# Four of 32 product chunks move a row or two later in a batched graph kernel

## The reference

```python
Ws = 0.5 * (W + jnp.swapaxes(W, -1, -2))
A = jax.nn.sigmoid(U @ U.T)
K = Ws * A[None, :, :]
deg = jnp.maximum(K.sum(axis=-1), EPS)
d = jax.lax.rsqrt(deg)
K = K * d[:, :, None] * d[:, None, :]
return w_scale * jnp.einsum('bnm,bmc->bnc', K, x)
# and around it
x = _layernorm(x + _L0_gnn_ref(x, adj, L0_gnn_U, L0_gnn_w_scale), axis=-1)
```

## Time and profile before

| | us |
|---|---|
| median of 3 runs | 486.6 |
| lowest and highest run | 481.2, 488.73 |
| the profiled execution, its own time | 489.78 |
| its span in the profile | 487.9 |

### The profile page before, as it was taken

How to read it: one execution, slowest core, us unless ns; L and a number is a source line. 1 busy time by engine, 2 the same in 40 slices (tenths; PEclk the granted TensorE clock), 3 DMA queues, 4 the chain that set the end, 5 groups by cost and what they waited for, 6 DMA issues and landing times.

```text
span 487.9 us, 14490 instructions
## 1 busy us (share of the span) xinstructions
PE 447.6 (92%) x5318; PEld 236.5 (48%) x5318; DVE 417.0 (85%) x1154; ACT 209.9 (43%) x655; POOL 113.4 (23%) x133
## 2 busy tenths in 40 slices
PE   7888899999989999999999999799998999899893
PEld 6556344555435553565354554454445544455352
DVE  6897467899699988999899998799889998799745
ACT  3886232554335442554335532454434542444420
POOL 0000011003330225103330234103330225103452
PEclk9996699999999999999999999999999999989998
DMA  8999299986999799996999699976999689984012
GB/s 290 387 330 350 81 362 368 359 301 221 358 343 324 259 321 362 375 326 236 362 380 358 212 380 364 351 241 244 387 345 343 261 322 361 356 253 170 2 41 47
DMA packets 101387, 143.11 MB, mean 293 GB/s; under 512 B 35824, under 2 KB 35824, under 8 KB 101360
## 3 DMA queue, kind: packets, MB, share of 16 engines
q1 hardware_dynamic: 86496, 139.01, 80.7%
q10 hardware_dynamic: 14864, 3.74, 3.6%
HBM read 138.54 MB, written 4.19 MB: 293 GB/s over the span
## 4 chain that ended last, share of the span: by engine, by line
PE 61%; DMA 14%; DVE 12%; issue 8%; ACT 2%; SPq 1%; POOL 0%; DVEq 0%; POOLq 0%
PE yp L437 35%; DMA k<-in_adj_dram 14%; PE tw L395 10%; PE kt L395 9%; DVE k L666 6%; DVE k L677 3%; PE yp L535 3%; PE yp L470 2%; ACT k L559 1%; ACT gate L546 1%; SPq L251 1%; DVE deg_parts L677 1%; DMA h<-in_L_gnn_U_dram 1%; PE kt L481 1%; PE kt L535 0%
## 5 line engine op out<-in xcount | busy, mean ns | idle before, releaser
L559 ACT ACTIVATE k<-kt 128x512 f32<-128x512 f32 (+3 forms) x288 | 149.5, 524 | 234.1 <-PE kt L395 233.8
L437 PE MATMUL yp<-k,z 128*64 128x512 f32 x944 | 239.6, 615 | 4.9 <-DVE z L697 2.6
L666 DVE TENSOR_TENSOR k<-tw,k 128x512 f32<-128x512 f32 (+2 forms) x320 | 193.4, 604 | 41.9 <-PE tw L395 28.5
L677 DVE CUSTOM_DVE_ANT_0 k<-k,gate 128x512 f32<-128x512 f32 (+2 forms) x320 | 198.5, 620 | 0.0
L395 PEld LDWEIGHTS kt<-ident,k 64*128 64x128 f32 x1920 | 75.4, 142 | 86.3 <-issue 86.1
L395 PEld LDWEIGHTS tw<-ident,k 64*128 64x128 f32 x2176 | 83.5, 141 | 67.0 <-issue 65.7
L395 PE MATMUL kt<-ident,k 64*128 64x64 f32 x1920 | 94.2, 232 | 19.5 <-DVE deg_parts L677 13.5
L395 PE MATMUL tw<-ident,k 64*128 64x64 f32 x2176 | 101.7, 230 | 4.5 <-DMA k<-in_adj_dram 1.7
L437 PEld LDWEIGHTS yp<-k,z 128*64 128x64 f32 x944 | 56.4, 137 | 73.1 <-issue 60.0
L327 POOL TENSOR_TENSOR d<-deg,minus_half 128x4 f32<-128x4 f32 x32 | 32.5, 1015 | 222.1 <-DVE deg L687 221.4
L559 ACT ACTIVATION_READ_ACCUMULATOR k<-kt 128x1 f32 x288 | 57.2, 198 | 0.0
(11 more groups left out here) (53 smaller groups left out, 138.7 us busy)
## 6 DMA issues: line engine op xcount, KB each, us to landing
k<-in_adj_dram SPq DMA_DIRECT2D x128, 1024.0 KB, 7.4
xt<-in_x_dram ACTq DMA_DIRECT2D x7, 512.0 KB, 7.6
out_dram<-h SPq DMA_DIRECT2D x7, 512.0 KB, 7.0
xt<-in_x_dram SPq DMA_DIRECT2D x1, 512.0 KB, 14.5
out_dram<-k SPq DMA_DIRECT2D x2, 128.0 KB, 2.1
out_dram<-k SPq DMA_DIRECT2D x3, 64.0 KB, 1.7
h<-in_L_gnn_U_dram SPq DMA_DIRECT2D x1, 128.0 KB, 3.2
out_dram<-k ACTq DMA_DIRECT2D x1, 64.0 KB, 1.9
```

What stands on the lines that cost most here:

```text
L437: t = pe.matmul(yp[at:at + C, m // 2, :], z[:, n * G + c, :], K[(n, m)][:, c, :], start=(q == first_unit[m] and c == 0), stop=(q == last_u ...
L559: nc.scalar.activation(K[(j, i)][:, r, c0:UW].rearrange("p (c h e) -> p c h e", h=2, e=H), whole_rows(kt[:, 0:2, :], r % 2, (UW - c0) // P ...
L666: nc.vector.tensor_tensor(row, whole_rows(tw[:, tw_bank[g] // 2 * 2:tw_bank[g] // 2 * 2 + 2, :], g % 2, w // P), row, ALU.add).then_inc(su ...
L677: nc.vector.tensor_tensor_reduce(row, row, A[:, A_AT[g]:A_AT[g] + w], 1.0, 0.0, ALU.mult, ALU.add, deg_parts[:, i * G + r, j:j + 1]).then_ ...
```

## The change

Four numbers of the table change, one or two rows each: chunk 27 goes from row 56 to 58, chunk 28 from 59 to 60, chunk 29 from 61 to 62, and chunk 31, the last one, from 65 to 66. Chunk 30 stays in row 64.

```diff
-PRODUCT_ROWS = [29, 29, 32, 32, 33, 33, 35, 35, 38, 38, 39, 39, 42, 44, 44, 45, 45, 45, 46, 46, 46, 47, 50, 52, 54, 56, 56, 56, 59, 61, 64, 65]
+PRODUCT_ROWS = [29, 29, 32, 32, 33, 33, 35, 35, 38, 38, 39, 39, 42, 44, 44, 45, 45, 45, 46, 46, 46, 47, 50, 52, 54, 56, 56, 58, 60, 62, 64, 66]
```

## The result

| | before | changed |
|---|---|---|
| median, us | 485.64 (4 runs) | 500.0 (4 runs) |
| lowest and highest, us | 481.2, 488.73 | 497.02, 502.63 |
| profiled execution, its own time, us | 489.78 | 497.02 |
| its span, us | 487.9 | 495.2 |
| its mean granted clock | 0.971 | 0.982 |

The ratio is 1.0285, with a 95% interval of 1.023 to 1.034. The forecast was 494.7 us, 1.7% slower, with a range up to 499: the sign was right, the time lies outside. The two profiled executions lie only 7.2 us apart, because that of before, taken apart from its four runs, was slower than each of them, and that of the changed kernel was the fastest of its four. So the profiles show where time goes, and the runs how much it is.

What follows compares the result with a forecast made beforehand. VectorE and TensorE bound the kernel in turn, with row 68's unit load just in time. Late loads of +8.9 us less 0.8 gave +8.1 us on a median of 486.6: 494.7 us, 1.7% slower, range 486 to 499.

Steps and rivals of the forecast that it cites:

- What bounds the kernel: VectorE limits one stretch of each element, TensorE the next; unit (3,2)'s load for row 68 lands just as needed.
- the ring of TensorE, load, VectorE: TensorE's products lead to a load, then VectorE, then TensorE; a late load is passed on one for one.
- Chunk 31's shift of 1.30 us: Row 66's tw and y transposes delay chunk 31 and group 7's load issue by 1.30 us, bounds 1.2 to 1.5.
- The wait at row 68: VectorE's add of row 68 waits 1.0 to 1.5 us for its load in all seven elements.
- Chunk 27 and ScalarE at no cost: Group 6's later loads and ScalarE's later second y copy cost 0; uncovered, at most 6.3 and 0.7 us.
- The 0.8 us back from the transposes of row 60: VectorE gets these transposes a chunk earlier, saving waits of 0.48 and 0.32 us in two elements: -0.8 us.
- 7 x 1.3 - 0.2 = +8.9: Seven late loads for row 68, 1.3 us each, less 0.2 us spare: +8.9 us, bounds +8.2 to +10.3.
- the clock, which I costed at 0 behind row 70's wait: TensorE's new 1.3 us wait at row 70 was taken not to lower the clock: 0 us.
- much slower: Idle time at row 70 lowers the clock in each of 7 elements: 11.9 us more, 506.6 us; chance 0.06.
- faster: A shorter stretch without products before row 58's kt keeps the clock up; 482.4 us with the load hidden; chance 0.07.
- The hidden load: Row 68's load stays hidden, only the 0.8 us gain is left: 485.8 us, half hidden 490; chance 0.18.

Runs made afterwards that it cites:

- only31_prey: Only chunk 31 moved from row 65 to 66, ahead of the four y transposes, against the kernel before: ratio 1.0071.
- only31: Only chunk 31 moved from row 65 to 66, behind the y transposes, against the kernel before: ratio 1.0264.
- only27_29: Chunks 27, 28 and 29 moved as in the change, chunk 31 left in row 65, against the kernel before: ratio 1.0013.
- after_again: The changed kernel, unedited, timed and profiled a second time beside the kernel before: ratio 1.0261.

## Why the prediction was wrong, step by step

**What bounds the kernel**: right. The load of unit (3,2) was on the edge, and the ring of TensorE, load, VectorE passes a delay on one for one. In `only31_prey`, `only31` and the changed kernel row 70's `kt` waits as long as the add of row 68, within 0.04 us, in the six elements beside the second. From VectorE's add of row 40 to the same add an element later, the shortest elements take 53.6 us before, 54.8 in the changed kernel and 54.7 in `only31`, where 1.2 us more were forecast.

**Chunk 31's shift of 1.30 us**: 1.34 measured. **The wait at row 68**: forecast 1.0 to 1.5 us in all seven elements; six have 0.94 to 1.29. Against 1.05 us of such waits that the kernel before already had, these six add 5.8 us, a little under the 7.6 of my sum, because the later loads were quicker: from issue to the add it is 5.10 to 5.34 us now, and was 5.32 to 5.59.

**Chunk 27 and ScalarE at no cost**: right, `only27_29` is at 1.0013. **The 0.8 us back from the transposes of row 60**: not seen in the total, although the waits at row 60 went.

**The step that failed** is the term "7 x 1.3 - 0.2 = +8.9", taken as the price of seven equal elements with nothing beside it but -0.8. Two things were left out of it.

The first is the second element. With the term's 1.3 us for it I had no reason but that the others looked alike. It waits 5.25 us in the first profile, 2.17 in the second and 1.67 in `only31`. That brings the waits of row 68 to 12.1, 9.5 and 8.2 us, which is 11.0, 8.5 and 7.2 more than before, around the 8.9 of the term. The row that could have warned me is thin: the kernel before lists "issue" among what TensorE waited for, with 2.2 us at the products and 1.7 us at the `tw` transposes, but all of it except 1 us stands ahead of 60 us, and only 0.34 us of it lies in that element. That the first turn of new code is not steady could be asked; the size could not be read.

The second is the clock, which I costed at 0 behind row 70's wait. The mean granted clocks, 0.982 in the changed kernel's profile and 0.971 before, hide it. In the second element of the first profile the clock was 0.50 for 3.4 us from 173.8 us on, right behind the `kt` that had waited 3.35 us. In `after_again` it fell behind a wait of 1.57 us in the sixth element (timeline, and busy time by windows):

```profile
396.36 0.72 PE L395 MATMUL kt<-ident,k 64*128 64x64 f32 x16 [1.57 <-DVE deg_parts L677]
...
397.21 3.48 PE L437 MATMUL yp<-k,z 128*64 128x512 f32 x8
...
401.35 1.94 PE L437 MATMUL yp<-k,z 128*64 128x512 f32 x8
...
397.50:400.90 3.40, 3.40 (x14) 0.78 (x12) 3.40 (x10) 0.89 (x4) 1.42 (x2) 0.50 0.00 0
```

The same work takes 3.48 us there and 1.94 a little later, 1.5 us more. So the rival "much slower" did happen in part: in one element of seven in each of these two profiles, not in all, and in none of `only31`. The rival "faster" did not happen.

Added up, waits and clock give 12.5 us in the first profile and 10.0 in the second. The ratios 1.0285 and 1.0261 are 13.8 and 12.7 us. That of `only31`, 1.0264, is 12.9 us beside 7.2 us of waits. So 1 to 6 us remain open, most where the second element had the least surplus, and the second element is not the whole answer. Part of the rest may again be the clock: the mean over an execution was 0.955 to 0.965 in the four runs of `only31` and 0.960 to 0.986 in those of the kernel before beside them. No run here holds the clock and moves the chunk alone, so this stays a candidate. Without the increments the same change costs 7.6 us and its waits 7.7, which is about what I had forecast.

**The hidden load** is refuted by all profiles. By the Trainium skill, "DMA: Bandwidth & Descriptors", section "Anatomy of one DMA — SWDGE (gpsimd) path", a transfer of one unit would take 4.4 us, as an estimate, and the change would cost 2.8 us. That formula is for transfers issued by GpSimd; here SP issues them, no whole unit's load for row 68 landed in under 4.9 us in any profile, and the change cost 13.8 us.

## What to carry to other kernels

- A buffer's release is an event with a consumer far away. Before moving an instruction that counts a release up, measure issue to use against issue to landing for the transfer behind it; a move of one row cost 2.6% here since that margin was nearly nil.
- A moved instruction should be followed through the passes that are not steady, too: first turn, unrolled head, tail. One element of seven had a fifth to over two fifths of the waits here.
- A longer wait can cost more than its length, when the clock falls behind it. The mean clock of an execution does not show that; the clock of the stretch behind the wait does.
- To show that a chain is the cause, free the dependency and leave the order alone. Regrouping the units did, and also showed that a second, unintended cost (both matmuls in one column half) can hide the answer.

## What the runs showed of the hardware

- Two fp32 matmuls of 64 x 512 in different column halves of TensorE's array overlap: 1.08 us for a chunk, 1.93 us if both are in one half.
- The granted clock fell to 0.50 for 3.4 us, once for 6.8, at the end of long waits of TensorE at row 70 or within 1 us of it: at eight of the nine waits of 2.38 to 4.19 us over all profiles, at four of the ten of 1.52 to 1.77 us, and at none of the shorter ones.
- In row 66 of the loop's first turn TensorE pauses for 0.6 to 2.6 us, waiting for nothing that the profile shows. The place is after the seventh transpose in six of the eight profiles of kernels with chunk 31 behind those transposes and the increments in place, and after the third in five of the eight with it ahead; the others have no such pause. That they are waits for code is inferred.
- A unit load of 1 MB for row 68, issued as the DMA engines run dry, took 5.0 to 5.5 us to land in the kernel before and in six of seven elements of the changed one, and 6.85 in its second. Half of it took 4.3 to 4.6 us in six elements, only 0.7 us less.
- Removing 42 semaphore increments from TensorE's program made the kernel before 1.4% faster (0.5 to 2.2%). Why is open.
